# A routed two-expert layer on one core: normalising the second pass per half quad

## The reference, cut to what matters

```python
x = x + gnn(layernorm(x), adj)                 # first part, not touched by the change
z = layernorm(x)                               # [128, 128, 128]: 16384 tokens of width 128
logits = z @ gate_w + gate_b                   # 16 experts
topk_vals, topk_idx = top_k(logits, 2); w = softmax(topk_vals)
h   = relu(z @ w1[e] + b1[e])                  # 256 wide, for each of the two experts
moe = sum_k w[k] * (h_k @ w2[e_k] + b2[e_k])
y   = z + moe
out = x + (y - mean(y)) / sqrt(var(y) + 1e-5) * gamma + beta
```

## Time and profile before

| | before |
|---|---|
| median of 3 runs | 710.54 us (709.33 to 710.82) |
| the profiled execution's own time | 710.99 us |
| span of the profiled execution | 709.0 us |
| time outside the span | 1.99 us |
| mean granted TensorE clock | 0.888 |
| first part, then first pass (TensorE busy until) | about 289 us, 458 us |
| second pass, from its first transposes | 499.6 us to the end |
| busy: PE, DVE, ACT, POOL | 544.5, 539.0, 407.8, 466.6 us |

### The profile page before, as it was taken

One profiled execution on the slowest core, in us unless ns is written; L12 is line 12 of the kernel. 1 busy time (PEld: TensorE's weight loads), 2 busy tenths in 40 slices (PEclk: granted clock), 3 DMA queues, 4 the chain that ended last, 5 costly groups with the idle time before them and its releaser, 6 DMA issues.

```text
span 709.0 us, 18043 instructions
## 1 busy us (share of the span) xinstructions
PE 544.5 (77%) x4140; PEld 486.8 (69%) x4140; DVE 539.0 (76%) x2791; ACT 407.8 (58%) x1345; POOL 466.6 (66%) x526
## 2 busy tenths in 40 slices
PE   1766789887888873399999999800799999999920
PEld 1655566665666652399999999800789999999920
DVE  5988599897997997288888888700299999999950
ACT  2889655454554540266666666500588888888810
POOL 3666647675765767067777777776067777777774
PEclk9989999897987985599999999955799999999975
DMA  8999649432332313379885665430997676664110
GB/s 216 282 281 282 158 147 278 143 104 75 96 94 84 97 49 114 80 210 334 258 251 192 202 190 185 150 149 28 294 328 231 191 215 202 208 203 142 49 49 7
DMA packets 115098, 121.40 MB, mean 171 GB/s; under 512 B 19017, under 2 KB 99613, under 8 KB 115008
## 3 DMA queue, kind: packets, MB, share of 16 engines
q1 hardware_dynamic: 95936, 76.79, 38.7%
q0 software_dynamic: 17920, 43.03, 16.7%
q10 hardware_dynamic: 1152, 0.56, 0.3%
HBM read 68.67 MB, written 55.90 MB: 176 GB/s over the span
## 4 chain that ended last, share of the span: by engine, by line
PE 38%; POOL 7%; ACT 7%; issue 4%; DMA 1%; DVE 1%; SPq 1%; POOLq 0%; ACTq 0%; DVEq 0%
PE bank L987 19%; PE bank L1003 15%; ACT hs L1055 4%; POOL rows_by_second L222 4%; POOL out_dram L222 3%; PE bank L976 3%; ACT xT L1036 2%; PE bank L1000 2%; DMA R<-rows_by_second 0%; DMA rows_by_second<-R 0%; DMA R<-rows_by_first 0%; ACT wr L1044 0%; SPq L912 0%; ACT L1064 0%; SPq L914 0%
## 5 line engine op out<-in xcount | busy, mean ns | idle before, releaser
L222 POOL DMA_INDIRECT rows_by_second<-R x144 | 146.2, 1015 | 62.2 <-issue 36.6
L222 POOL DMA_INDIRECT out_dram<-R x144 | 143.2, 994 | 66.7 <-issue 38.7
L1055 ACT ACTIVATE hs<-bank,wr 128x128 f32<-128x128 f32 x432 | 127.5, 368 | 86.7 <-PE bank L987 82.7
L1003 PE MATMUL bank<-W,hs 128*128 x1152 | 176.1, 289 | 0.0
L222 POOL DMA_INDIRECT rows_by_first<-st x128 | 125.3, 979 | 76.6 <-ACT st L546 40.2
L987 PE MATMUL bank<-xT,wr 128*128 128x128 f32 x1152 | 159.1, 282 | 7.2 <-ACT xT L1036 6.7
L1003 PEld LDWEIGHTS bank<-W,hs 128*128 128x128 f32 x1152 | 151.7, 192 | 3.5
L987 PEld LDWEIGHTS bank<-xT,wr 128*128 128x128 f32 x1152 | 143.1, 196 | 14.6 <-ACT xT L1036 13.4
L1124 DVE SCALAR_TENSOR_TENSOR R<-bank,R 128x128 f32<-128x128 f32 x288 | 87.6, 346 | 66.6 <-PE bank L1003 63.2
L1044 ACT COPY wr<-W1b 128x258 f32 x288 | 105.0, 427 | 14.7 <-PEq L858 14.7
L554 ACT ACTIVATE HT<-bank,bcol 128x128 f32<-128x128 f32 x128 | 46.7, 365 | 69.6 <-PE bank L455 65.7
(11 more groups left out here) (137 smaller groups left out, 875.4 us busy)
## 6 DMA issues: line engine op xcount, KB each, us to landing
R<-rows_by_second SPq DMA_DIRECT2D x144, 196.0 KB
R<-rows_by_first SPq DMA_DIRECT2D x144, 68.0 KB
xq<-in_x_dram SPq DMA_DIRECT2D x32, 256.0 KB, 4.0
aq<-in_adj_dram SPq DMA_DIRECT2D x32, 256.0 KB, 5.0
x2r<-in_x_dram SPq DMA_DIRECT2D x32, 256.0 KB, 2.9
rows_by_second<-filler SPq DMA_DIRECT2D x1, 3136.0 KB, 13.7
rows_by_second<-filler SPq DMA_DIRECT2D x16, 196.0 KB
rows_by_second<-R POOLq DMA_INDIRECT x144
```

Of the source, the lines that this page charges most:

```text
L222: return nc.gpsimd.indirect_dma_start(dst, bass.IndirectOffsetOnAxis(ap=idx, axis=0), src, None, bounds_check=limit[n], oob_is_err=False)
L1003: i = mm(o, hs[:, h, c, k * P:(k + 1) * P], W2[:, bass.ds(e[k], 1), c, :].rearrange("p o f -> p (o f)"), start=False, stop=c == 1, skip_gr ...
L1055: i = a(hs[:, h, c, k * P:(k + 1) * P], ps_h[c][h][:, k * P:(k + 1) * P], ACT.Relu, bias=wr[:, u % 2, 2 * h + k, F + c:F + c + 1])
```

## The change

In the second pass, normalisation and the release of scatters go by half quads instead of quads. `norm_a(G, h)` has 2 bn_stats, 2 bn_aggr and the multiplication by gamma for its half; the memset and the addition of epsilon are gone. `norm_b(G, h)` has a reciprocal and two multiply-adds. `root(G, h)` reads the variances where bn_aggr wrote them and adds epsilon as the bias of the activation. `e_fin` counts halves, and GpSimd waits for it before blocks 0 and 2. One square root of a constant is issued at the start of ScalarE's passes. The order on VectorE and on ScalarE changes as the diff shows.

```diff
@@ GpSimd, quad
-                            if j == 0:
-                                hold(pool, e_fin, G - NQUAD + 1)
+                            if j % 2 == 0:
+                                hold(pool, e_fin, 2 * (G - NQUAD) + j // 2 + 1)
@@ ScalarE
                 act.wait_ge(tables, 1)
                 act.wait_ge(r_w, 16 * 5)
+                a(scrap[:, :], eps_ln[:, 0:1], ACT.Sqrt)
...
-                def root(G):
-                    n = G - NQUAD
-                    act.wait_ge(e_ve, n + 1)
-                    if not (isinstance(n, int) and n < 1):
-                        act.wait_ge(e_rs, n)
-                    a(fsd[:, :], fve[:, :], ACT.Sqrt).then_inc(e_sd, 1)
+                def root(G, h):
+                    n = 2 * (G - NQUAD) + h
+                    act.wait_ge(e_ag, n + 1)
+                    if not (isinstance(n, int) and n < 2):
+                        act.wait_ge(e_rs, n - 1)
+                    a(fsd[:, h, :], fmv[:, 2 * h:2 * h + 2, 1], ACT.Sqrt, bias=eps_ln[:, 0:1]).then_inc(e_sd, 1)
@@ ScalarE, quad
                     relu(r, G, u, 0)
+                    if r == 1 and not start:
+                        root(G - 1, 0)
                     if not last:
                         weights(r, q + 1, G + 1, v, 0, e[0])
                         weights(r, q + 1, G + 1, v, 1, e[1])
+                    if r == 1 and not start:
+                        root(G - 1, 1)
                     relu(r, G, u, 1)
                     if not last:
                         turn_out(G + 1, v)
                         weights(r, q + 1, G + 1, v, 2, e[2])
                         weights(r, q + 1, G + 1, v, 3, e[3])
-                    if r == 1 and not start:
-                        root(G - 1)
                     if last and r == 1:
-                        root(G)
+                        root(G, 0)
+                        root(G, 1)
@@ VectorE
-                def norm_a(G, u):
-                    m = G - NQUAD
-                    hold(dve, e_acc, 2 * G + 2)
-                    for j in range(QUAD):
+                def norm_a(G, u, h):
+                    n = 2 * (G - NQUAD) + h
+                    hold(dve, e_acc, 2 * G + h + 1)
+                    for j in range(2 * h, 2 * h + 2):
                         i = v.bn_stats(fst[:, j, :], R[:, u, j, C_Y:W_B])
                     i.then_inc(e_bn, 1)
-                    hold(dve, e_bn, m + 1)
-                    v.memset(scrap[:, :], 0.0)
-                    for j in range(QUAD):
+                    hold(dve, e_bn, n + 1)
+                    for j in range(2 * h, 2 * h + 2):
                         i = v.bn_aggr(fmv[:, j, :], fst[:, j, :])
                     i.then_inc(e_ag, 1)
-                    dve.wait_ge(e_ag, m + 1)
-                    v.tensor_scalar(fve[:, :], fmv[:, :, 1], LN_EPS, None, ALU.add).then_inc(e_ve, 1)
-
-                def norm_b(G, u):
...
-                    dve.wait_ge(e_sd, m + 1)
-                    v.reciprocal(frs[:, :], fsd[:, :]).then_inc(e_rs, 1)
...
+                    y = R[:, u, 2 * h:2 * h + 2, C_Y:W_B]
+                    v.tensor_tensor(y, y, gm_bc[:, :].rearrange("p (o d) -> p o d", o=1).broadcast_to([P, 2, P]),
                                     ALU.mult).then_inc(e_f1, 1)
...
+                def norm_b(G, u, h):
...
+                    hold(dve, e_sd, n + 1)
+                    v.reciprocal(frs[:, h, :], fsd[:, h, :]).then_inc(e_rs, 1)
+                    hold(dve, e_rs, n + 1)
+                    hold(dve, e_f1, n + 1)
+                    for k in range(2):
...
@@ VectorE, quad
                     if not start:
                         share(r, G - 1, before, 1)
                         if r:
-                            norm_a(G - 1, before)
+                            norm_b(G - 1, before, 0)
+                            norm_a(G - 1, before, 1)
...
                     share(r, G, u, 0)
+                    if r:
+                        norm_a(G, u, 0)
                     if r and not start:
-                        norm_b(G - 1, before)
+                        norm_b(G - 1, before, 1)
                     if last:
                         share(r, G, u, 1)
                         if r:
-                            norm_a(G, u)
-                            norm_b(G, u)
+                            norm_b(G, u, 0)
+                            norm_a(G, u, 1)
+                            norm_b(G, u, 1)
```

More of the change, by code:

```diff
@@ L867, in build @@
         fmv = sb("fmv", [P, QUAD, 2])
-        fve = sb("fve", [P, QUAD])
-        fsd = sb("fsd", [P, QUAD])
-        frs = sb("frs", [P, QUAD])
+        fsd = sb("fsd", [P, 2, 2])
+        frs = sb("frs", [P, 2, 2])
         e_beta = sem("e_beta")
@@ L874, in build @@
         e_sc = [sem(f"e_sc{i}") for i in range(RING)]
-        e_z, e_zt, e_xe, e_wc, e_h, e_r0, e_r1, e_o, e_acc, e_bn, e_ag, e_ve, e_sd, e_f1, e_f2, e_fin, e_rs = (
-            sem("e_" + k) for k in ("z", "zt", "xe", "wc", "h", "r0", "r1", "o", "acc", "bn", "ag", "ve", "sd", "f1",
+        e_z, e_zt, e_xe, e_wc, e_h, e_r0, e_r1, e_o, e_acc, e_bn, e_ag, e_sd, e_f1, e_f2, e_fin, e_rs = (
+            sem("e_" + k) for k in ("z", "zt", "xe", "wc", "h", "r0", "r1", "o", "acc", "bn", "ag", "sd", "f1",
                                     "f2", "fin", "rs"))
@@ L1139, in norm_a @@
                         i = v.bn_aggr(fmv[:, j, :], fst[:, j, :])
                     i.then_inc(e_ag, 1)
-                    dve.wait_ge(e_ag, m + 1)
-                    v.tensor_scalar(fve[:, :], fmv[:, :, 1], LN_EPS, None, ALU.add).then_inc(e_ve, 1)
-                def norm_b(G, u):
-                    m = G - NQUAD
-                    y = R[:, u, :, C_Y:W_B]
-                    v.tensor_tensor(y, y, gm_bc[:, :].rearrange("p (o d) -> p o d", o=1).broadcast_to([P, QUAD, P]),
-                                    ALU.mult).then_inc(e_f1, 1)
-                    dve.wait_ge(e_sd, m + 1)
-                    v.reciprocal(frs[:, :], fsd[:, :]).then_inc(e_rs, 1)
[L1152 to L1157, removed]
+                    y = R[:, u, 2 * h:2 * h + 2, C_Y:W_B]
@@ new lines, in norm_a @@
+                    v.tensor_tensor(y, y, gm_bc[:, :].rearrange("p (o d) -> p o d", o=1).broadcast_to([P, 2, P]),
+                                    ALU.mult).then_inc(e_f1, 1)
+                def norm_b(G, u, h):
+                    n = 2 * (G - NQUAD) + h
+                    hold(dve, e_sd, n + 1)
[3 more added lines that the diff above has]
+                    for k in range(2):
+                        y = R[:, u, 2 * h + k, C_Y:W_B]
+                        i = v.scalar_tensor_tensor(out=y, in0=y, scalar=frs[:, h, k:k + 1],
+                                                   in1=R[:, u, 2 * h + k, 0:P], op0=ALU.mult, op1=ALU.add)
```

## The result

| | before | after |
|---|---|---|
| median | 710.54 us (5 runs, 709.24 to 710.82) | 746.87 us (5 runs, 745.09 to 748.06) |
| ratio | | 1.0513, 95% interval 1.0492 to 1.0533 |
| profiled execution: time, span | 710.99, 709.0 us | 745.30, 741.6 us |
| mean granted clock | 0.888 | 0.905 |

The forecast was 748 us with a range of 741 to 765. The kernel is 5.1% slower, and the time is 1.1 us from the forecast.

What follows compares the result with a forecast made beforehand. GpSimd's scatters bound the second pass; after the change a 6.4 us quad loop would. 34 loops reach 724.5 us, plus 22.1 is a 746.6 span; 1.99 outside it, less 0.45 to the median, gives 748 us, range 741 to 765.

Steps and rivals of the forecast that it cites:

- The loop: Second pass, per quad: root(G-1, 1) delays relu(G, 1) by 1.51 us, so the loop grows from 4.87 to 6.38 us.
- the low bound: Second-pass loop: 6.25 us a quad, if VectorE's independent instructions overlap by 0.04 to 0.08 us at two or three joints.
- The sum: Whole kernel: first(37, 0) at 506.92, 34 loops of 6.4 to 724.5, plus 22.1 us, a span of 746.6 us.
- the tail: From first(71, 0) to the end of the span: last scatter ends at 15.9, plus 6.2 us, together 22.1 us.
- The time outside the span: Profiled time over its span: 1.99 us, carried over from the kernel before, giving 748.6 us.
- GpSimd: Second-pass scatters: the first at 511.4, 4.6 us sooner; then POOL waits in each quad and the loop is the bound.
- The covers: Table load hidden in ScalarE's 4.95 us idle before the passes; VectorE's extra work hidden in 0.9 us to spare a quad.
- The first, a falling clock: Second pass on PE: longer idle lowers TensorE's clock, 12 to 13 us more, 760 us; chance 0.23.
- the prediction's own sign: Profile after: a 6.4 us quad with the clock below 1.00 between 520 and 720 us means the clock falls in addition.
- The rival on the other side: Second pass: half 1's variance comes in time, POOL stays the bound and starts 4.6 us sooner, 706 us; chance 0.07.

Runs made afterwards that it cites:

- e1: Kernel after, with the root of half 1 moved behind relu(G, 1), turn_out(G+1) and both pairs of weight copies; 707.66 us, ratio 0.9955 to before.
- e3: Kernel after, with norm_a(G-1, 1) ahead of norm_b(G-1, 0) on VectorE; 727.52 us, ratio 1.0235 to before.
- e4: Kernel after, with root(G-1, 1) moved between relu(G, 1) and turn_out(G+1); 711.08 us, ratio 0.9998 to before.
- e6: e1 without the line that loads the square root's table early; 709.14 us, ratio 0.9973 to before.
- e2: Kernel before, with its one root(G-1) for four blocks moved ahead of relu(G, 1); 751.71 us, ratio 1.0566 to before.
- e5: Kernel before, with one square root of a constant added where ScalarE's passes begin, loading the table there; 708.64 us, ratio 0.9978 to before.

## Why the prediction was right, point by point

**The loop.** It was put at 6.38 and taken as 6.4; the trace has 6.32 to 6.36. The joints of it are within about 0.1 us of the paper: bn_aggr ends at t = 4.48 (paper 4.58), `relu(G, 1)` starts at 4.71 (paper 4.71; 4.68 in a quad of 6.33 us). Small errors cancelled there. VectorE's overlap, which I had kept for the low bound, did happen (0.08 between multiply-add and bn_stats, 0.09 between share and reciprocal), and the root is 0.29 long instead of 0.24. It now has a bias that is read from a tile; that this is the reason was not isolated. The two holds between reciprocal and multiply-add took 0.10 (582.48 + 0.15 to 582.73), where 0.03 was reckoned.

**The sum.** Forecast span 746.6, measured 741.6. Of the 5.0 us, 3.2 are the start of the second pass: `first(37, 0)` at 503.68, not 506.92. Of these, 1.9 are there before the first pass (its first `turn_out` at 293.06, not 294.94). No instruction of the change stands between there and `first(37, 0)`; in the traces of the other kernels this instant lies anywhere from 506.0 to 510.0. Another 1.3 us are the loop, 6.36 on the mean of 34: most quads are 0.07 shorter than the 6.4, and the two of 6.50 and 7.22 give 1.1 us of that back. And 0.5 are the tail (719.96 to 741.6 is 21.6, forecast 22.1). The time outside the span went the other way, 3.7 us against the 1.99 that I had carried over. That was a term missed, not noise: its median is 3.1 to 3.6 us in every kernel with halves (after, e1, e3, e4, e6) and 1.9 in every one without (before, e2, e5); why stays open. So part of the closeness is luck: the terms of the change inside the span were right to about 2 us, and the early start of the pass and the missed term cancelled in part.

**GpSimd.** The first scatter was put 4.48 us behind `first(37, 0)` and came 4.48 behind (503.68 to 508.16). It idles once in every quad for 1.30 us, where 0.30 us lie between other scatters, and the bound had changed hands as forecast.

**The covers.** The table's load is hidden where it stands now: 3.92 us of idle time are left behind it. VectorE's extra work is hidden behind its waits of 1.22 us a quad. The two halves of gamma take 0.39 us each, so the split costs 0.07 us against the row of 0.71, or 0.10 against the 0.68 that most quads have, where the prediction's estimate was 0.16. That the change's other parts cost nothing and even gain is shown by e1.

**The rivals.** The first, a falling clock, was there once, not for a quarter of the time. From 520 to 720 us the clock stayed at 1.00 but for one stretch at 0.96, with 1.6 us idle in each quad and PE busy 0.72 to 0.77 of the time. So by the prediction's own sign, a clock below 1.00 between 520 and 720 us, this rival holds in addition, but the fall cost 0.9 us of the 12 to 13 that it had. The rule of the Trainium skill that spoke for this rival (TensorE: Matmul & The Clock Gate, A second HAM failure mode) tells of a clock that swings; here it fell once in 32 quads. In the traces of the kernel before, e1, e3 and e4 it is 1.00 all the way from 520 to 680 us, and e2, which idles as long as the kernel after, has one fall as well (0.96 over 640 to 680). The rival on the other side, that the variance comes in time, was wrong as a forecast and right as a description of what a better order brings: 706 us by its sum, 707.7 in e1. Its condition, that the loop stay under GpSimd's pace, is just what e1 meets and e4 misses by 0.11 us.

## What to carry to other kernels

Before a wait is put into an engine's program, look at what stands behind it: here an instruction of 0.3 us, placed ahead of the critical work, cost 39 us, and behind that work it cost nothing. Finer release of work helps only if each finer step's inputs come before the point where its engine would block; write the loop out from one quad's rows with t = 0 at its start, and the new loop's length can be had closely: here to 0.05 us for the change and e2, and to 0.14 and 0.2 for e3 and e4, where the overlaps and dependencies at the joints were not redone. When an engine paces a pass, as GpSimd did, every microsecond by which it starts earlier counts, and the others together have a slack that can be worked out, beyond which they become the bound.

## What was not expected of the hardware

The activation with a bias from a tile, on 2 elements, took 0.295 to 0.312 us in the kernel after, against 0.205 to 0.243 for 4 elements without in the one before. The first scatter of each half 0 took 1.12 us instead of 0.97, and its start fell within VectorE's multiplication by gamma in 34 of the 36 quads:

```profile
577.68 0.39 DVE L1144 TENSOR_TENSOR R<-R,gm_bc 128x256 f32<-128x256 f32 x1
577.79 1.12 POOL L222 DMA_INDIRECT out_dram<-R  x1 [0.39 <-issue]
```

No run was made for this, but the other traces speak for the overlap as the cause and not the place in the quad. In the other two quads that scatter took 0.97 us. In e4 it starts within gamma only in the first quad and takes 1.12 us there, and 0.97 in the other 35. In e2, whose gamma is 0.68 us long, 31 scatters start within one, and take 1.38 us at the median. By what means VectorE holds GpSimd up is not shown.

PE's clock was also steadier than I had allowed for. In the first part it was 0.88 over 40 us in which PE was busy for 0.85 of the time; in this loop, with 0.72 to 0.77, it fell once in 200 us. What tells the two apart stays open.
